# Decoder layer: the prologue by token rows, and the folding of attention weights inside the scan steps

## The reference

```python
# 1 Mamba block; here the scan runs over the 8 rows, and the 128 tokens are its batch
x, z = split(in_proj(h)); x = silu(causal_conv4(x))       # 512 channels each
dt_r, B, C = split(x_proj(x))                             # 128, 16, 16
delta = softplus(dt_proj(dt_r) + b);  A = -exp(A_log)     # A: 512 x 16
for t in range(8):
    state = exp(delta_t * A) * state + (delta_t * u_t) * B_t    # 512 x 16 per token
    y_t = sum_n state * C_t
out = out_proj((y + u * D) * silu(z))
# 2 cross-attention to ctx (64 features), 16 heads, rotary on q and kv
q = rope((x Wq) w_kcq);  scores = (q W_qr) . (rope(ctx) W_kr);  softmax
out = (softmax @ kv) w_kckv @ Wo
# 3 feed-forward: Hadamard transform, 8 bit activations, ternary weights, relu^2
```

## Time and profile before

| | |
|---|---|
| median of 3 runs | 562.46 us (562.05 to 563.54) |
| the profiled execution: its time, its span | 561.04 us, 559.2 us |
| TensorE, matmuls | busy 451.7 us, 81% |
| VectorE | 408.5 us, 73% |
| ScalarE | 319.8 us, 57% |
| GpSimd | 238.5 us, 43% |
| DMA | 29.89 MB, mean 53 GB/s; 296 and 301 GB/s in the first two fortieths of the span |
| chain that ended last | PE 39%, DVE 24%, issue 19%, ACT 7%, POOL 6%, DMA 3% |
| landing, w_q (2 MB) | 11.7 us after its issue |

### The profile page before, as it was taken

The page is one execution under the profiler, slowest core; times in us unless marked ns, Lnnn a source line. Parts: engine busy times, 40 slices in busy tenths (PEclk is TensorE's granted clock), DMA queues, the critical chain, the costliest instruction groups (busy, mean ns, idle before and its releaser), DMA issues.

```text
span 559.2 us, 10332 instructions
## 1 busy us (share of the span) xinstructions
PE 451.7 (81%) x3272; PEld 372.0 (67%) x3280; DVE 408.5 (73%) x733; ACT 319.8 (57%) x700; POOL 238.5 (43%) x165
## 2 busy tenths in 40 slices
PE   5999966448657747667899999999999999997833
PEld 2437766345546637546788988898988988896612
DVE  0947998089999999999654576777777676676443
ACT  1539748788888888888234353434535353434310
POOL 2300563397797897986123223322232223322010
PEclk9999978757758668777999999999999999999665
DMA  8721684421011101111200000000000000000000
GB/s 296 301 75 40 182 256 163 175 60 39 29 45 40 28 28 39 36 38 28 80 11 2 10 2 2 19 0 19 0 19 0 9 9 0 19 0 19 1 10 10
DMA packets 19268, 29.89 MB, mean 53 GB/s; under 512 B 1712, under 2 KB 14384, under 8 KB 18288
## 3 DMA queue, kind: packets, MB, share of 16 engines
q1 hardware_dynamic: 19248, 29.64, 15.8%
HBM read 23.34 MB, written 6.29 MB: 53 GB/s over the span
## 4 chain that ended last, share of the span: by engine, by line
PE 39%; DVE 24%; issue 19%; ACT 7%; POOL 6%; DMA 3%; DVEq 2%; POOLq 0%; SPq 0%; ACTq 0%
PE ps L361 34%; DVE ps L1113 7%; DVE reg_b L1120 4%; POOL reg_b L958 2%; POOL reg_b L937 2%; DVE ps L1110 2%; PE ps L558 2%; POOL small L942 1%; ACT reg_b L816 1%; DVE reg_b L1173 1%; DMA reg_a<-w_kr 1%; DMA reg_a<-a_log 1%; DVE x1T L1059 1%; DVE reg_b L1172 1%; PE ps L464 1%
## 5 line engine op out<-in xcount | busy, mean ns | idle before, releaser
L937 POOL TENSOR_TENSOR reg_b<-reg_c,reg_a 128x1024 f32<-128x1024 f32 x56 | 130.3, 2370 | 18.1 <-ACT reg_a L724 17.6
L958 POOL TENSOR_TENSOR reg_b<-reg_b 128x768 f32<-128x768 f32 x32 | 58.0, 1812 | 140.1 <-DVE reg_b L1173 107.4
L464 PE MATMUL ps<-ident,hc 128*128 128x128 f32 x452 | 83.9, 340 | 24.2 <-ACT hc L740 23.8
L361 PE MATMUL ps<-x1T,Mw 128*128 (+1 forms) x768 | 93.5, 278 | 0.0
L740 ACT ACTIVATE hc<-reg_b,bc 128x512 f32<-128x512 f32 x112 | 80.2, 716 | 23.3 <-PE ps L464 11.5
L464 PEld LDWEIGHTS ps<-ident,hc 128*128 128x128 f32 x452 | 66.0, 176 | 39.2 <-ACT hc L740 39.2
L361 PEld LDWEIGHTS ps<-x1T,Mw 128*128 128x128 f32 x768 | 88.2, 192 | 3.4 <-DVE reg_b L1173 0.3
L1120 DVE SCALAR_TENSOR_TENSOR reg_b<-reg_c,bc,ps 128x512 f32<-128x512 f32 x112 | 82.8, 745 | 0.0
L816 ACT ACTIVATE reg_b<-ps,small 128x128 f32<-128x128 f32 x128 | 45.3, 366 | 40.0 <-DVE small L1178 39.3
L1113 DVE TENSOR_TENSOR ps<-ps,reg_b 128x512 f32<-128x512 f32 x96 | 66.5, 698 | 0.0
L731 ACT ACTIVATE ps<-reg_b 128x512 f32<-128x512 f32 x112 | 64.9, 581 | 0.0
(11 more groups left out here) (141 smaller groups left out, 743.2 us busy)
## 6 DMA issues: line engine op xcount, KB each, us to landing
reg_a<-a_log SPq DMA_DIRECT2D x4, 1024.0 KB, 5.6
reg_a<-w_q SPq DMA_DIRECT2D x1, 2048.0 KB, 11.7
zs_dram<-reg_c SPq DMA_DIRECT2D x4, 512.0 KB, 3.3
ud_dram<-Nw SPq DMA_DIRECT2D x4, 512.0 KB, 4.9
reg_a<-w_o SPq DMA_DIRECT2D x1, 2048.0 KB, 11.0
ud_t<-ud_dram SPq DMA_DIRECT2D x8, 256.0 KB, 2.7
zs_t<-zs_dram SPq DMA_DIRECT2D x8, 256.0 KB, 2.6
reg_a<-w_kcq SPq DMA_DIRECT2D x1, 1536.0 KB, 14.9
```

The source lines that it names most:

```text
L361: return pe.matmul(o, l, r, start=start, stop=stop)
L464: return pe.matmul(o, src, ident[:, :], start=start, stop=stop, is_transpose=True, skip_group_check=True)
L937: pool.tensor_tensor(dA[:, g % RING], delta_r[:, bass.ds(t, 1), :].to_broadcast([P, SA, DI]), Abc[:, g * SA:(g + 1) * SA, :], ALU.mult).th ...
L958: pool.tensor_tensor(rq[:, g % 2].rearrange("p a c n -> p (a c n)"), pc[:, g % 2].rearrange("p a c n -> p (a c n)"), psn[:, g % 2].rearran ...
```

## The change

The folding jobs leave the prologue. A second list, `side`, has 28 of them in smaller pieces: P in 4, KV in 2, N in 6, M in 16 (one head each), in this order, four per scan step, each in one PSUM bank (5 or 7, in turn). TensorE does them after the sums of states 0, 4, 8 and 10, ScalarE evicts them after its iterations 5, 9, 13 and 15. The weights of M come through a ring of two buffers (`mring`). The loops of TensorE, ScalarE and SyncE over the scan steps are unrolled. The transposed x1 moves from bank 7 to the second half of bank 6.

The prologue works by token rows: DT and UD have the tokens of two steps as their stationary operand, so delta and the skip term come out in token rows without a turn; only u is still transposed (TU). VectorE adds the bias, spread over the partitions by DMA, and makes delta and delta times u itself; ScalarE's Abs reads the result from SBUF. A_log is exponentiated once in a 128 x 64 form, written to DRAM, and spread from there. The order of the jobs and of the evictions changes. GpSimd's memsets are gone: zeros for Nw come by DMA, and N contracts over 64 partitions.

```diff
+PE_SIDE = (0, 4, 8, 10)
+ACT_SIDE = (5, 9, 13, 15)
-        jobs = row("X", *range(CI)) + row("Z", 0, 1) + row("FF", 0) + row("DTR", 0)
-        jobs += row("DT", *range(CI)) + row("BC", 0) + row("UD", *range(CI)) + row("BCT", 0) + row("M", 0, 1, 2, 3)
-        jobs += row("Z", 2, 3) + row("M", 4, 5, 6, 7)
-        jobs += row("KV", 0) + turns(0) + row("N", *range(QC)) + turns(1, 2, 3) + row("P", 0, 1)
-        by_act = ("Z", "DTR", "N", "P", "TDELTA", "TDU", "UD")
+        jobs = row("X", *range(CI)) + row("Z", 0) + row("DTR", 0) + row("FF", 0) + row("DT", 0, 1) + row("BC", 0)
+        jobs += row("DT", 2) + row("BCT", 0) + row("DT", 3) + row("UD", 0, 1, 2) + row("Z", 1, 2, 3) + row("UD", 3)
+        jobs += row("TU", *range(T // 2))
+        by_act = ("Z", "DTR", "UD")
+        side = row("P", *range(4)) + row("KV", 0, 1) + row("N", *range(2 * QC)) + row("M", *range(NH))
+        side_pos = {job: j for j, job in enumerate(side)}
+        per_step = len(side) // (T - 1)
...
+        def side_bank(job):
+            return ps[:, 5 + 2 * (side_pos[job] % 2), :]
```

```diff
+            sp.wait_ge(ae_s, 1)
+            sp.dma_start(a_dram.rearrange("n d -> (n d)").rearrange("(p j) -> p j", p=P), a_c).then_inc(a_out, 16)
+            sp.dma_start(bdt_bc, b_dt.partition_broadcast(P)).then_inc(ld["bdt"], 16)
...
+            sp.wait_ge(a_out, 16)
+            for g in range(NST // NA):
+                sp.dma_start(Abc[:, g * NA:(g + 1) * NA, :],
+                             a_dram[g * NA:(g + 1) * NA].rearrange("n d -> (n d)").partition_broadcast(P)
+                             ).then_inc(ld[f"abc{g}"], 16)
...
+            store_skip(0)
+            store_skip(1)
+            store_skip(2)
+            for p in range(1, CI):
+                store_gates(p)
+            store_skip(3)
+            sp.wait_ge(pe_job, pos[("Z", CI - 1)] + 1)
+            sp.dma_start(nw_flat, zeros).then_inc(ld["zero"], 16)
+            load_m(0)
+            load_m(1)
```

```diff
+            def side_job(j):
+                job = side[j]
+                kind, c = job
+                o = side_bank(job)
+                need(pe, side_e, j - 1)
...
+                elif kind == "P":
+                    once(ld["wo"], 32)
+                    for i in range(2):
+                        for e in range(2):
+                            h = 2 * (2 * c + i) + e
+                            last = mm(o[e * DC:(e + 1) * DC, i * DM:(i + 1) * DM],
+                                      kckv_s[:, h * DC:(h + 1) * DC], wo_s[:, h, :])
...
+                elif kind == "M":
+                    m = c // 2
+                    once(ld[f"m{m % 2}"], 32 * (m // 2 + 1))
+                    w = mring[:, m % 2, :]
+                    for k in range(KM):
+                        last = mm(o[:, k * DQ:(k + 1) * DQ], w[:, c % 2 * DM + k * P:c % 2 * DM + (k + 1) * P],
+                                  w[:, 2 * DM + c % 2 * DQ:2 * DM + (c % 2 + 1) * DQ])
+                last.then_inc(side_m, 1)
...
-            with pe.Fori(1, T) as t:
+            for t in range(1, T):
                 skip_sum(t)
                 for n in range(NST):
                     state_sum((n + 1) % WRING, NST * (t - 1) + n + 2, n == NST - 1)
+                    if n in PE_SIDE:
+                        side_job(per_step * (t - 1) + PE_SIDE.index(n))
                     if n == 3:
                         out_proj(t - 1)
```

```diff
             squares_of(0)
+            skips(0)
             squares_of(1)
+            skips(1)
+            skips(2)
+            squares_of(2)
+            gates(1)
             gates(2)
             gates(3)
+            skips(3)
+            squares_of(3)
...
+            def take_side(j):
+                act.wait_ge(side_m, j + 1)
+                if kind == "KV":
...
+                    if n in ACT_SIDE:
+                        take_side(per_step * (t - 1) + ACT_SIDE.index(n))
```

```diff
+                dve.tensor_tensor(delta_r[:, 2 * p:2 * p + 2, :], pair(("DT", p)),
+                                  bdt_bc.to_broadcast([P, 2, DI]), ALU.add).then_inc(dve_free, 1)
...
+                dve.scalar_tensor_tensor(delta, delta, 0.0, e, ALU.max, ALU.add).then_inc(delta_s, 1)
...
+            def step_inputs(p):
+                take(("TU", p))
+                dve.wait_ge(delta_s, p + 1)
+                dve.tensor_tensor(step_pair(du_r, p), flat(("TU", p)), step_pair(delta_r, p), ALU.mult
+                                  ).then_inc(dve_free, 1)
...
+            softplus(1)
+            step_inputs(0)
             softplus(2)
+            step_inputs(1)
             softplus(3)
+            step_inputs(2)
+            step_inputs(3)
```

More of the change, by code:

```diff
@@ L70, in decoder_layer @@
                   w_q, w_kcq, w_qr, w_kr, w_kckv, w_o, ctx_kv, w_up, w_dn,
-                  ident_c, rope_q, rope_kv, had, out, zs_dram, ud_dram, x1_dram):
+                  ident_c, rope_q, rope_kv, had, zeros, out, zs_dram, ud_dram, x1_dram, a_dram):
     with ExitStack() as stack:
@@ L404, in _ @@
                 elif kind == "DTR":
[L405 removed]
                     once(ld["xp"], 32)
[L407 to L408 removed]
+                    for k in range(CI):
+                        pe.wait_ge(silu_s, k + 1)
+                        for half in range(2):
                             last = mm(o[:, half, :], wxp_s[:, k, 0:RANK],
@@ L510, in _ @@
                         turn_x1(t - 1)
+            pe.wait_ge(side_e, len(side))
             def project(t, g):
@@ L679, in take, with last_tap @@
                 act.wait_ge(pe_job, pos[job] + 1)
-            act.wait_ge(ld["small1"], 48)
-            for c in range(CI):
+            act.wait_ge(ld["alog"], 16)
+            act.activation(a_c, a_c, ACT.Exp).then_inc(ae_s, 1)
+            act.wait_ge(cst, 1)
+            act.activation(spare, neghalf, ACT.Silu).then_inc(act_passed, 1)
+            act.wait_ge(ld["convw"], 16)
+            def last_tap(c):
                 take(("X", c))
@@ L685, in _, with gated @@
                                scale=convw_s[:, c, CONV - 1:CONV]).then_inc(tap3, 1)
-            for c in range(CI):
+            def gated(c):
                 act.wait_ge(dve_free, freed[("X", c)][1])
@@ L693, in gates @@
                 act.activation(zs_st[:, p % 2, :], flat(("Z", p)), ACT.Silu).then_inc(act_free, 1)
+            last_tap(0)
+            last_tap(1)
+            gated(0)
+            last_tap(2)
+            gated(1)
+            last_tap(3)
+            gated(2)
             gates(0)
-            gates(1)
+            gated(3)
             take(("DTR", 0))
             act.activation(dtr, flat(("DTR", 0)), ACT.Copy).then_inc(act_free, 1)
-            for c in range(CI):
-                take(("DT", c))
-                act.activation(E[:, c, :], flat(("DT", c)), ACT.Abs, bias=bdt_s[:, c:c + 1]).then_inc(abs_s, 1)
@@ L762, in _ @@
                       2: [((0, 32), 3, lo, lo), ((32, 64), 3, hi, hi), ((64, 128), 3, hi, hi)]}
-            for c in range(QC):
-                if c == 1:
-                    squares_of(3)
-                take(("N", c))
-                src = flat(("N", c)).rearrange("p (x n) -> p x n", n=P)
-                for (p0, p1), tile, dst, frm in pieces[c]:
-                    last = act.activation(nv[p0:p1, :, tile, dst], src[p0:p1, :, frm], ACT.Copy)
-                last.then_inc(act_free, 1)
@@ L975, in step_kT @@
             def step_kT(t):
+                if isinstance(t, int) and t == 0:
+                    pool.wait_ge(side_e, side_pos[("KV", 1)] + 1)
                 need(pool, smm, G * t)
@@ L1073, in _ @@
                             ).then_inc(dve_free, 1)
+            biased(3)
+            softplus(0)
             dve.wait_ge(dve_free, freed[("BCT", 0)][1])
             dve.tensor_tensor(cb_n[:, :], bc[:, 0, 0:NST], bc[:, 0, NST:2 * NST], ALU.mult).then_inc(cb_s, 1)
-            for p in range(4):
-                take_query_products(p)
+            ternary(1, wdn_raw, wdnq[:, :, :])
             dve.wait_ge(cb_s, 1)
```

370 lines of the change are left out of this document (171 added, 199 removed).

## The result

The changed kernel takes 568.43 us (median of 4 runs, 566.67 to 571.99) against 562.25 us (562.02 to 563.54) for the kernel before in the same measurement: a ratio of 1.0113, with the 95% interval 1.0059 to 1.0167. It is slower by 1.1%, which is small, but the interval leaves out 1. The prediction was 571.6 us.

What follows compares the result with a forecast made beforehand. VectorE alone was taken to set the scan step. 561.04 us less 24.0 for the prologue plus 33.2 of scan waits gave 570.2 profiled; 1.4 more made the median 571.6, its own range 564 to 578.

Steps and rivals of the forecast that it cites:

- loss by GpSimd in softplus(3): Prologue: GpSimd's first two argument products lie on VectorE's softplus(3) and cost 0 to 4.7 us, taken as 3.5.
- first state operation; gain: End of prologue: the scan starts at 90.1 instead of 114.06 us, a gain of 24.0, bounds 19 and 27.5.
- first wait, M step: Scan, iteration 5: the eviction waits for a job behind the gate, delaying state 6's exponential; VectorE loses 3.5 us.
- second wait, M step: Scan, iteration 9: ScalarE waits for the side job after state 4, delaying decay 10; 1.0 us lost (0.6 to 1.5).
- P step: Scan step with P side jobs: VectorE loses 4.2 us at the first wait and 1.5 at the second, 5.7 together.
- KV step: Scan step with KV side jobs: VectorE loses 3.2 us at the first wait and 0.8 at the second, 4.0 together.
- N step: Scan step with N side jobs: VectorE loses 4.2 us at the first wait and 1.3 at the second, 5.5 together.
- The last step: Whole kernel: the median of before's runs lies 1.4 us above its profiled execution, so 570.2 becomes 571.6.
- The clock rises: Rival, scan: side jobs keep TensorE at full clock, waits total 24.2 us, time 562.6, give or take 4; chance 0.15.
- The waits are covered: Rival, scan: ScalarE's spare 3.3 us per step absorbs the evictions, VectorE stays at 22.1; 538.5 us; chance 0.08.
- Weak: Rival, prologue: it gives only 14 us because squares, gates and stores in one queue hold up TU; 581 us; chance 0.10.
- strong prologue: Rival: the prologue gives 27.5 us and only iteration 5 waits, 7 times 3.5 = 24.5; 559.5 us; chance 0.07.

Runs made afterwards that it cites:

- the kernel with GpSimd held: GpSimd's first argument products wait for the last delta instead of the first, against the kernel with TensorE's first two side jobs ahead of skip_sum: 535.57 us.
- The useless matmuls in the gap: Changed kernel plus, in M steps, the first side job's matmuls run twice more, unused, ahead of skip_sum: 563.55 us, ratio 1.0017.
- two jobs ahead of the gate: Changed kernel with TensorE's first two side jobs of each step moved ahead of skip_sum, ScalarE's evictions in place: 538.29 us, ratio 0.9571.
- both changes of the prologue: TU 0 and 1 early and GpSimd held until the last delta, against the kernel with two side jobs ahead of skip_sum: 534.69 us.
- the rates as before: Raw a_log spread, four exponentials on ScalarE behind its last squares, against the kernel with two side jobs ahead of skip_sum: 539.63 us.
- the one with the last stores: ScalarE copies skip pair 3 before gate 3, against the kernel with TU 0 and 1 early and GpSimd held until the last delta: 536.45 us.

## Why the prediction was right, point by point

**The structure held.** The place of the evictions behind the jobs that they wait for decides, VectorE loses the time, one operation pair after each gate, and attention keeps its length. A step between two M gates took 25.6 us (206.87 to 232.47), where 22.1 plus 4.5 had been forecast. The timeline of one M step:

```profile
206.87 0.68 DVE L1175 TENSOR_TENSOR yT<-ps,zs_t 128x512 f32<-128x512 f32 x1
...
207.60 1.11 PE L497 MATMUL ps<-ident,ud_t 128*128 128x128 f32 x4 [3.48 <-DVE yT L1175]
...
208.51 1.06 PE L497 MATMUL ps<-ident,hc 128*128 128x128 f32 x4
...
209.36 1.49 PE L386 MATMUL ps<-mring 128*128 128x192 f32 x4
...
210.89 0.49 ACT L839 ACTIVATE Mw<-ps 128x384 f32<-128x384 f32 x1 [4.44 <-PE ps L386]
211.27 0.59 ACT L779 ACTIVATE ps<-reg_b 128x512 f32<-128x512 f32 x1
...
211.90 0.70 DVE L1160 TENSOR_TENSOR ps<-ps,reg_b 128x512 f32<-128x512 f32 x1 [3.10 <-ACT ps L779]
```

It is to be read downwards as a chain: gate, skip sum, sum 0, job, eviction, exponential, decay. ScalarE had been idle since 206.45, 0.4 us before the gate.

**The terms.**

| step of the prediction | forecast | measured |
|---|---|---|
| VectorE free for softplus(0) | 44.8 | 45.2 |
| `gates(1)` done | 66.5 | 66.8 |
| `step_inputs(0)` starts | 67.8 | 68.8 |
| GpSimd's first product | 78 | 77.3 |
| loss by GpSimd in softplus(3) | 3.5 | 3.5 |
| first state operation; gain | 90.1; 24.0 | 90.8; 23.3 |
| first wait, M step | 3.5 | 3.0 to 3.1 |
| second wait, M step | 1.0 | 0.3 |
| four M steps | 18.0 | 13.4 |
| P step | 4.2 + 1.5 | 3.8 + 0.5 |
| KV step | 3.2 + 0.8 | 2.8 + 0.7 |
| KV step, iterations 13 and 15 (N jobs) | 0 | 0.8 + 0.4 |
| N step | 4.2 + 1.3 | 4.1 + 2.7 + 0.7 + 0.4 |
| all waits of the scan | 33.2 | 30.4 |
| VectorE's own work, the rest | 0 | 1.2 |
| attention | 0 | -0.3 |

The total came closer than its terms. Measured against the forecast the M steps were 4.6 us lower and the P step 1.4, the N step 2.5 higher and the KV step 0.7; the prologue gained 0.7 less, and VectorE's own work took 1.2 more. That these errors cancel to about 1 us is luck. What the forecast had right by its own working is the structure and the first wait.

*First wait.* Forecast 5.38 us from the gate to the decay of state 6; measured 211.90 - 206.87 = 5.03. The loss is 3.1 us (3.10 in the row). The eviction came at 4.02 instead of 4.26, and from exponential to VectorE it took 0.63 instead of 0.70.

*Second wait: mis-sized.* I had sum 4 at 9.0 and the job seen at 9.9 us after the gate, with ScalarE there from 9.3 on and 1.0 us lost. Measured are 8.7 for the sum, 9.4 for the job, ScalarE there at 9.0. The term was a small difference of times 10 us away from the gate, which were 0.3 to 0.5 us off, and came out three times too large. It was the largest error, 4 x 0.7 of the 4.6 us by which the M steps came out lower.

*The N step: mis-sized the other way.* I said that iterations 13 and 15 cost nothing and the second wait 1.3 us. What I had not seen is that TensorE's clock stays low for longer in this step. From 155.91 to 158.70 it was granted 0.50 and over the output projection 0.61, where an M step has 0.80 from 210.87 to 214.50, its projection included. Whether the four matmuls of N and their eviction in pieces keep it low, no run shows. The projection took 3.08 us, 1.89 in the earlier trace rows and in all M steps, and the second decay waited 2.71:

```profile
158.71 3.08 PE L386 MATMUL ps<-w_out_s,yT 128*128 128x256 f32 x8
...
164.85 0.70 DVE L1160 TENSOR_TENSOR ps<-ps,reg_b 128x512 f32<-128x512 f32 x1 [2.71 <-ACT ps L779]
```

*The prologue.* The turn that waits for Z1's banks, hence for `squares_of(2)`, a table load and `gates(1)`, ended 1.0 us late. I had its transposes at 0.95 us; from 66.76 to 68.82 TensorE's matmuls took 2.01 us at a granted clock of 0.50. The wait stands in the trace, and the undisturbed lengths behind it:

```profile
68.82 1.23 DVE L1115 TENSOR_TENSOR reg_c<-ps,reg_c 128x1024 f32<-128x1024 f32 x1 [7.50 <-PE ps L456]
69.96 0.69 DVE L1103 TENSOR_SCALAR reg_b<-reg_b 128x1024 f32<-128x1024 f32 x1
70.68 3.74 DVE L1105 SCALAR_TENSOR_TENSOR reg_b<-reg_b 128x1024 f32<-128x1024 f32 x3
...
78.00 2.18 DVE L1103 TENSOR_SCALAR reg_b<-reg_b 128x1024 f32<-128x1024 f32 x1
80.21 5.76 DVE L1105 SCALAR_TENSOR_TENSOR reg_b<-reg_b 128x1024 f32<-128x1024 f32 x3
...
88.41 2.35 DVE L1115 TENSOR_TENSOR reg_c<-ps,reg_c 128x1024 f32<-128x1024 f32 x2
```

```profile
77.26 2.36 POOL L973 TENSOR_TENSOR reg_b<-reg_c,reg_a 128x1024 f32<-128x1024 f32 x1 [54.79 <-DVE reg_c L1110]
79.57 2.80 POOL L973 TENSOR_TENSOR reg_b<-reg_c,reg_a 128x1024 f32<-128x1024 f32 x1
...
88.66 2.35 POOL L973 TENSOR_TENSOR reg_b<-reg_c,reg_a 128x1024 f32<-128x1024 f32 x1 [6.29 <-DVE reg_c L1110]
```

The collision cost (2.18 - 0.69) + (5.76 - 3.74) = 3.5 us, the value that I took between 0 and 4.7; the kernel with GpSimd held shows the same operations at their full speed, so it is caused by GpSimd and not by something else at that time. The operations at 88.41 have one operand in PSUM and ran beside a GpSimd product at their undisturbed 1.2 us each.

How the loss arises was wrong, though, and the right size was luck: I had a rate of 0.74 us per us of GpSimd. The ends of the operations show a stop instead. GpSimd's first product ends at 79.62, and VectorE's operation from 78.00 (0.69 us of its own) at 80.18; the second product ends at 82.37, and the first of the next three, taken by itself, is this:

```profile
80.21 3.25 DVE L1105 SCALAR_TENSOR_TENSOR reg_b<-reg_b 128x1024 f32<-128x1024 f32 x1
```

It ends at 83.46, 1.09 us after the product, and has some 1.25 us of its own. So each operation of VectorE stood almost until GpSimd's product was over and then ran at full speed, and the loss is what was left of the two products when they came: 79.62 - 78.00 and 82.37 - 80.21, together 3.8 us, of which 3.5 were lost. The second product stood in turn: it took 2.80 us instead of 2.36. The row from before says the same (75.20 + 2.66 and 75.70 + 3.24 are 1.1 us apart). The rule that I set beside it, in the Trainium skill, "SBUF — State Buffer", section "SBUF: two separate sides", gives the engine that starts first the shared ports for its whole instruction, while the other blocks fully. The trace agrees; my "whole 4.7" was a misreading of the rule, since an operation that comes late stands only for the rest.

**The last step.** I added 1.4 us, because the median of before lay so far above its profiled execution. For the changed kernel the median (568.43) lies 1.0 below the profiled one (569.41). Against the profiled execution the sum was 0.8 us off (570.2); the forecast of 571.6 was 3.2 off the median. The difference of a median to one execution is scatter of single runs, and no property to carry over.

**The rivals.** *The clock rises*: it didn't. From the gate at 206.87 on for 4 us it was

```profile
206.87:210.87 4.00, 3.27 (x14) 3.18 (x15) 1.93 (x4) 0.00 (x0) 3.98 (x2) 0.50 0.21 66
```

that is 1.2 GHz, and before the change 0.54. The useless matmuls in the gap show that the rival's mechanism exists, and that its price, 1.3 us for an M step (4.5 less 3.2), was nearly right: a first wait shrank from 3.0 to 1.6. The Trainium skill, "TensorE: Matmul & The Clock Gate", section "What's actually happening", lets activity release the throttle; that kernel agrees with it in three M steps, while a fourth stayed at 0.57. *The waits are covered*: not in this order; with two jobs ahead of the gate they are, at 538.29 us, and the rival's price had been 538.5. Its condition was put rightly, but the side of it that decides, whether TensorE has the job done before ScalarE comes to it, can be met on TensorE as well as on ScalarE. *Weak* and *strong prologue* both fall by 90.8.

## What to carry to other kernels

In this scan an eviction put into an in-order queue cost what it waited for, not what it took. Work off the critical path belongs on the producing engine before the dependency that makes it late (here in TensorE's idle time ahead of the gate, the longest wait in the earlier trace rows), or its consumer far enough behind it; ask of every added wait how many results the bounding engine has in stock, here two exponentials. And when one such stop is taken away, compute the next one anew, since the first had been hiding it.

## What had not been expected of the hardware

The attention stage, the same instructions in the same order, has no single length: it took 290.1 to 290.8 us in nine of the thirteen profiles of this study (before and the change among them), 287.3 and 287.4 us in two (both changes of the prologue; the rates as before), and 288.7 and 289.0 in the other two. The same stretch of it, first in the version with both, then in the one with the last stores:

```profile
468.96:500.96 32.00, 26.12 (x243) 22.59 (x242) 20.51 (x48) 14.78 (x51) 7.06 (x7) 1.00 0.03 9
```

```profile
467.56:499.56 32.00, 26.55 (x232) 22.45 (x230) 20.33 (x48) 13.60 (x49) 7.06 (x7) 0.94 0.03 9
```

TensorE's granted clock falls earlier in the second, and some 10 matmuls less are done in 32 us. What decides when it falls is open; it wasn't tried apart. It is the reason why 1.4 us won at the start of the scan could end as 1.4 us lost, and a gain of that size in an early stage can't be read from the total alone.

The loss by GpSimd depended on the operands. In the same prologue operations wholly in SBUF were stretched, those with a PSUM operand were not, and GpSimd's own product beside such an operation kept its 2.35 us too.
